# Unread matmuls placed ahead of six of TensorE's waits

## The chip, the cores and the metric

The kernel runs on one core of a Trainium2 chip (trn2). The metric is the device time of one execution in microseconds (us); lower is better. "PE" is TensorE's matmul queue, "PEld" its weight loads, DVE is VectorE, ACT is ScalarE, POOL is GpSimd and SPq the queue of transfers that SyncE issues.

## The reference, cut to what matters

The input is 16 batches of 512 tokens with 128 features. Three residual blocks follow each other; each starts with a layer norm.

- Block 1: linear attention with Chebyshev features. q, k, v = x W_in, clipped; polynomials of orders 1 to 5; running sums of T(k) v and of T(k) along the tokens; out = numerator / (denominator + 1e-7), times W_out.
- Block 2: a second layer norm, then ordinary causal softmax attention with 16 heads of 8 features, times Wp.
- Block 3: a gate picks 2 of 8 experts for each token; each expert is 128 to 512, exact gelu, 512 to 128; the two results are added with softmax weights.

```python
x = x + _L0_attn_ref(_layernorm(x), W_in, W_out)
x = x + _L0_ffn_ref(_layernorm(x), ...)      # softmax attention, then the experts
```

## The kernel before

All five engines run programs written out by hand, each a sequence of steps with waits on semaphores. An engine goes through its steps strictly in the written order.

**The pipeline over batches.** `pipelined(body)` runs `body` 21 times, t = -5 to 15. One pass works on up to six batches at once, each at another stage: `f` (block 1's norm and projections), `h` (its running sums and result), `g` (block 2's norm and projections), `m` (the row maxima of the scores), `b` (exp and the product with the values) and `t` (Wp, the gate, the dispatch to the experts). In the first five passes only some stages have a batch. This is the run-up: pass -5 has f only, pass -4 has h and f, pass -3 has g, h and f, pass -2 has m as well, and so on. Inside a pass TensorE's steps stand at 129 numbered places; `MAX_PE`, `SCORES_PE` and `VALUES_PE` list the places of the maxima, scores and value products.

**Steps of TensorE that matter here** (line numbers of the profile):

- `turn_h` (L1254, place 75): four transposes of the normed batch (L1243) into PSUM bank `front0`, behind a wait for the norm on DVE; then `project_k`, `project_q`, `project_v` (L1264, places 79 to 81): three f32 products of 128 x 512.
- `head_sums` (L1281, places 4 and 6, matmuls L1289): per-head sums of the k polynomials, then of the q polynomials. Both wait for POOL's even orders (`t24`, L1125 and L1126) and DVE's odd ones.
- `denominators` (L1293, place 51, matmuls L1297): eight matmul instructions of 16 columns; it waits for the fourth running sum on DVE. `turn_rden` (L1303), `spread_rden` (L1313) and `output1` (L1324) follow from it.
- `turn_ln`, `project_q2`, `project_k2`, `project_v2` (places 58 to 70, L1338 to L1346): block 2's projections.
- `maximum` (L1349, matmuls L1360 and the mask L1362): 44 steps for a batch (`NMAX` = 44), n = 0 to 43. Step 0 and step 22 (`NMAX // 2`) wait for a transfer that fills a half of the operand `stack`; the others wait until DVE has reduced the tile two steps back (L580). With `MAX_PE`, step 9 stands at place 39 and step 22 at place 83, two places behind `project_v`.
- `turn_x2` (L1434, place 25) and `gate` (place 31, L1441), then `ranks` (place 52, L1448 to L1452).
- After the 21 passes: a wait for the experts' plan and split weights, then `turn_in(0)` (four transposes L1243 of the first gathered block into `scores0`) and 39 expert blocks (`hidden` L1547, `output` L1559).

**Steps of DVE that matter here.** DVE's list `MAX_DVE` puts the reductions of steps 21, 22 and 23 one behind the other (slots 45 to 47); then come `third_order` (L513) and `fifth_order` (L517) of k, `max_rest` (L585), `ratio` (L561), and the other reductions. DVE too goes strictly in order.

The PSUM bank `scores1` (`ringE[1]`) is used by the scores and, later, by the experts' transposes.

Of the kernel before, what the change touches and what calls it, by code (L numbers as in the profile page):

```python
# [28 lines left out]
B, T = 16, 512  # L29
# [82 lines left out]
def block_kernel(nc, x, consts, cols, row_biases, w_in, w_out, wq, wk, wv, wp, gate_w, ew1, ew2, eb2, out):  # L112
    with ExitStack() as ctx:
        place = {}

        def sb(name, shape, dt=F32):
            tensor = ctx.enter_context(nc.sbuf_tensor(name, shape, dt))
            width = int(np.prod(shape[1:])) * (2 if dt == BF16 else 4)
            place[name] = nc.sbuf_base - -(-width // 32) * 32
            return tensor  # L120
# [22 lines left out]
        identb = sb("identb", [P, P], BF16)  # L143
        triu = sb("triu", [P, P], BF16)
        onesb = sb("onesb", [P, P], BF16)
        maskA = sb("maskA", [P, 4 * P], BF16)
# [111 lines left out]
        X, Y, Z, V = (ctx.enter_context(nc.psum_tensor(n, [P, T], F32)) for n in ("front0", "front1", "back0", "back1"))  # L258
        ringE = [ctx.enter_context(nc.psum_tensor(f"scores{i}", [P, T], F32)) for i in range(2)]
# [25 lines left out]
        NMAX = len(MAXIMA)  # L285
# [952 lines left out]
        def _(pe):  # L1238
            k = nc.tensor

            def turn(src, dst, done):
                for t in range(QT):
                    last = k.transpose(dst[:, t * P:(t + 1) * P], src(t), ident)  # L1243
                last.then_inc(done, 1)
# [6 lines left out]
            pe.wait_ge(W.const_ready, 4)  # L1251


            def turn_h(f, h, g):  # L1254
                pe.wait_ge(norm["a"]["out"], f * QT + QT)
                if g is not None:
                    pe.wait_ge(W.v_ev, g + 1)
                elif h is not None:
                    pe.wait_ge(W.rdT_ev, h + 1)
                turn(lambda t: hn[:, t, :], X, W.tr0)  # L1260
# [19 lines left out]

            def head_sums(f, z, dst, t24, t35, done, dst_read, upto):  # L1281

                if upto:
                    pe.wait_ge(dst_read, upto)
                pe.wait_ge(t24, f * 2 + 2)
                pe.wait_ge(t35, f * 2 + 2)
                for p in range(ORDERS):
                    j, var = (p, 0) if p < 4 else (0, 1)
                    last = k.matmul(dst[32 * j:32 * j + 32, :], cst[:, C_SUM + 32 * var:C_SUM + 32 * var + 32], z[p],  # L1289
                                    start=(p < 4), stop=(p > 0), skip_group_check=True)  # L1290
                last.then_inc(done, 1)

            def denominators(f):  # L1293
                pe.wait_ge(W.d_prod, f + 1)
                pe.wait_ge(W.kv_sum, f * ORDERS + 4)
                for t in range(QT):
                    last = k.matmul(X[:, t * H:(t + 1) * H], ksum[:, t * P:(t + 1) * P], cst[:, C_WS:C_WS + H],  # L1297
                                    start=True, stop=True)
                last.then_inc(W.den_mm, 1)
# [49 lines left out]
            def maximum(m, n, p):  # L1349

                head, heads, t = MAXIMA[n]
                if n in (0, NMAX // 2):
                    pe.wait_ge(stack_in[n // (NMAX // 2)], m * 32 + 32)
                if n == HALF_AT + 1:
                    pe.wait_ge(n2_ready[0], m + 1)
                elif n >= 2:
                    pe.wait_ge(W.smax_red, m * NMAX + n - (n != HALF_AT))
                for j in range(heads):
                    h, at = head + j, j * (t + 1) * P
                    k.matmul(ring(n)[:, at:at + (t + 1) * P], qst[p][0:MROW, h, t * P:(t + 1) * P],  # L1360
                             kst[p][0:MROW, h, 0:(t + 1) * P], start=(j == 0), stop=True, skip_group_check=True)
                k.matmul(ring(n)[:, 0:heads * (t + 1) * P].rearrange("p (h n) -> p h n", h=heads)[:, :, t * P:(t + 1) * P],  # L1362
                         identb[:, :], maskA[:, 0:heads * P].rearrange("p (h n) -> p h n", h=heads),
                         start=False, stop=True, skip_group_check=True).then_inc(W.smax_mm, 1)
# [67 lines left out]
                last.then_inc(W.o2_mm, 1)  # L1432

            def turn_x2(b):  # L1434
                pe.wait_ge(norm["b"]["out"], b * QT + QT)
                turn(lambda t: rows[:, 0, t, 0:D], Z, W.tr3)

# [25 lines left out]
            def body(t, b, m, g, h, f, p):  # L1463
# [3 lines left out]
                for n in range(SLOTS):  # L1467
                    at = lambda place, stage: n == place and stage is not None
                    if m is not None and n in MAX_PE:
                        maximum(m, MAX_PE.index(n), 1 - p)  # L1470
# [6 lines left out]
                    if at(4, h):  # L1477
                        head_sums(h, kx, X, W.k_t24, W.k_t35, W.ks_mm, W.x1_ready, h)
                    if at(6, h):
                        head_sums(h, qx, Y, W.q_t24, W.q_t35, W.qs_mm, *((W.x2_ready, t + 1) if t is not None else (W.outT_ready, h)))  # L1480
                    if at(25, t):
                        turn_x2(t)
                    if at(31, t):
                        gate(t)
                    if at(51, h):
                        denominators(h)
# [16 lines left out]
                    if at(75, f):  # L1503
                        turn_h(f, h, g)
# [21 lines left out]
            pipelined(body)  # L1526


            pe.wait_ge(W.plan_ready, 1)
            pe.wait_ge(W.wl_ready, 2 * E)  # L1530

# [76 lines left out]
```

## Time and profile before

| | |
|---|---|
| median of 3 runs | 1512.45 us (1511.88 to 1514.55) |
| the profiled execution | 1512.91 us |
| its span, first to last instruction | 1510.7 us |
| PE busy | 1260.2 us, 83% |
| DVE busy | 1167.6 us, 77% |
| ACT busy | 918.9 us, 61% |
| POOL busy | 854.2 us, 57% |
| chain that ended last | PE 61%, DVE 18%, issue 7%, ACT 6%, DMA 4%, POOL 3% |
| mean granted TensorE clock | 0.917 of full speed |

The chain is followed back from the last instruction, at each step to what released it; an engine's share of it is time that sets the end. The granted clock is 1.00 at 2.4 GHz and 0.50 at 1.2 GHz. A row of a timeline gives start, duration, engine, line, instruction, output and inputs, how many were merged, and in brackets the idle time of the engine before it with what ended it.

### The profile page before, as it was taken

What the parts mean: (1) busy time and instruction counts of PE and PEld (TensorE: products, weight loads), DVE (VectorE), ACT (ScalarE), POOL (GpSimd) and SP (SyncE); (2) the same over time, 40 slices, a digit from 0 to 9 for tenths busy, and PEclk for the clock granted to TensorE, in tenths of its full rate; (3) what the DMA queues carried; (4) which work ended last, traced back from release to release, by engine and by line L of the source; (5) the groups of instructions that cost most, each with busy time, mean ns of one, the idle gap of its engine ahead of it and who ended that gap; (6) DMA issues with size and microseconds to landing.
All of it is one profiled execution on the core that took longest, in us unless ns stands there. A gap on an engine that the chain in (4) does not pass through costs nothing.

```text
span 1510.7 us, 27693 instructions
## 1 busy us (share of the span) xinstructions
PE 1260.2 (83%) x8757; PEld 722.4 (48%) x8819; DVE 1167.6 (77%) x2654; ACT 918.9 (61%) x1794; POOL 854.2 (57%) x1077
## 2 busy tenths in 40 slices
PE   2545898999989999998999999989888199999970
PEld 0222354544545454454544545444445178888850
DVE  4548789888998988889898898875551578888864
ACT  1131376666767667675666766666545289999950
POOL 5567445766676666656766666552032326666660
PEclk9666799999999999999999999999999589999995
DMA  3012321404223141321403214043143022222238
GB/s 97 0 49 36 85 64 23 103 20 107 65 51 86 30 112 50 67 79 37 110 21 92 75 34 100 16 100 86 30 135 134 30 76 77 86 86 81 81 134 333
DMA packets 79345, 116.23 MB, mean 77 GB/s; under 512 B 15396, under 2 KB 61496, under 8 KB 74976
## 3 DMA queue, kind: packets, MB, share of 16 engines
q1 hardware_dynamic: 65888, 92.41, 23.4%
q0 software_dynamic: 9088, 17.33, 3.4%
q10 hardware_dynamic: 4224, 4.72, 1.0%
q8 instruction: 71, 1.16, 0.3%
q14 instruction: 74, 0.61, 0.1%
HBM read 58.29 MB, written 57.43 MB: 77 GB/s over the span
## 4 chain that ended last, share of the span: by engine, by line
PE 61%; DVE 18%; issue 7%; ACT 6%; DMA 4%; POOL 3%; SPq 1%; POOLq 0%; DVEq 0%; another core or an unknown queue 0%; ACTq 0%
DVE nm L580 9%; PE scores L1386 8%; PE front L1547 7%; PE back L1406 7%; PE back L1559 7%; PE maxima L1360 7%; PE front L1289 3%; PE front L1264 3%; ACT pr L963 3%; PE scores L1389 2%; PE back L1243 2%; PE maxima L1362 2%; DMA stack<-pairs 2%; DVE front L531 1%; PE front L1338 1%
## 5 line engine op out<-in xcount | busy, mean ns | idle before, releaser
L580 DVE TENSOR_REDUCE nm<-maxima 128x1 f32<-128x384 f32 (+3 forms) x704 | 427.7, 634 | 94.1 <-PE maxima L1362 67.3
L963 ACT ACTIVATE pr<-scores 128x384 f32<-128x384 f32 (+1 forms) x768 | 378.5, 524 | 186.4 <-PE scores L1389 172.3
L1360 PE MATMUL maxima<-stack 96*128 96x128 bf16 (+3 forms) x1024 | 258.2, 311 | 43.1 <-DVE nm L580 33.2
L1386 PE MATMUL scores<-stack 98*128 98x512 bf16 (+3 forms) x1024 | 260.7, 310 | 33.7 <-ACT pr L963 27.8
L1386 PEld LDWEIGHTS scores<-stack 98*128 98x128 bf16 x1024 | 91.7, 101 | 205.6 <-ACT pr L963 134.1
L1389 PE MATMUL scores<-maskB,identb 128*128 128x128 bf16 (+1 forms) x768 | 186.4, 243 | 0.0
L1406 PE MATMUL back<-pr,vaug 128*9 128x512 f32 (+3 forms) x2048 | 183.2, 454 | 0.0
L1164 POOL DMA_INDIRECT xg<-rows,sloti x128 | 129.9, 1014 | 88.4 <-DVE sloti L653 47.0
L1134 POOL TENSOR_TENSOR kv<-F,kv 128x512 f32<-128x512 f32 x80 | 112.5, 1418 | 116.2 <-DVE kv L534 116.2
L1360 PEld LDWEIGHTS maxima<-stack 96*128 96x128 bf16 x1024 | 85.8, 99 | 169.1 <-DVE nm L580 113.4
L1232 POOL DMA_INDIRECT pairs<-xs x104 | 111.0, 1067 | 78.8 <-DVE xs L814 52.0
L1362 PE MATMUL maxima<-maskA,identb 128*128 128x128 bf16 (+1 forms) x642 | 152.4, 237 | 0.0
L1547 PE MATMUL front<-h_first,w_now 128*128 128x512 f32 x312 | 126.3, 406 | 2.4 <-DVE h_second L794 2.4
L1099 ACT ACTIVATE xs<-front,b1p 128x512 f32<-128x512 f32 x156 | 107.4, 689 | 19.8 <-PE front L1547 16.7
L1125 POOL TENSOR_SCALAR F<-F 128x512 f32<-128x512 f32 x32 | 52.6, 1645 | 113.9 <-DVE F L513 113.9
L1559 PE MATMUL back<-hid_first,w_now 128*128 128x512 f32 x312 | 96.2, 390 | 0.0
L534 DVE TENSOR_TENSOR_SCAN kv<-one,front 128x512 f32<-128x512 f32 x80 | 95.2, 1206 | 0.1
L1145 POOL TENSOR_TENSOR kv<-kv 128x512 f32<-128x512 f32 x64 | 80.3, 1265 | 3.8 <-POOL kv L1145 0.4
L807 DVE TENSOR_TENSOR hid_second<-xs,hid_first 128x512 fp32r<-128x512 f32 x99 | 67.9, 686 | 15.6 <-ACT hid_first L1080 14.7
L1389 PEld LDWEIGHTS scores<-maskB,identb 128*128 128x128 bf16 x768 | 76.4, 99 | 6.9
L1080 ACT ACTIVATE hid_first<-xs 128x512 fp32r<-128x512 f32 x117 | 74.1, 633 | 3.7
L1362 PEld LDWEIGHTS maxima<-maskA,identb 128*128 128x128 bf16 x704 | 70.5, 100 | 8.7 <-issue 4.6
(223 smaller groups left out, 2491.7 us busy)
## 6 DMA issues: line engine op xcount, KB each, us to landing
stack<-spread SPq DMA_DIRECT2D x64, 384.0 KB, 6.4
spread<-qs SPq DMA_DIRECT2D x96, 128.0 KB
spread<-ks SPq DMA_DIRECT2D x96, 128.0 KB
xs<-xg SPq DMA_DIRECT2D x39, 272.0 KB, 2.9
stack<-pairs SPq DMA_DIRECT2D x8, 1024.0 KB, 16.6
xg<-xs SPq DMA_DIRECT2D x17, 272.0 KB
xs<-in_x SPq DMA_DIRECT2D x16, 256.0 KB, 5.8
acc<-xs SPq DMA_DIRECT2D x16, 256.0 KB, 2.3
```

What stands on the lines that cost most here:

```text
L580: v.tensor_reduce(nm[:, h:h + heads, t], ring(n)[:, 0:heads * (t + 1) * P].rearrange("p (h n) -> p h n", h=heads), AX.X, ALU.max, negate=T ...
L963: a.activation(pr[:, n % PR, 0:width], ringE[n % 2][:, 0:width], ACT.Exp).then_inc(W.exp_ready, 1)
L1134: g_.tensor_tensor(kv[:, p, :], qx[p], kv[:, p, :], ALU.mult).then_inc(W.qk_prod, 1)
L1164: g_.indirect_dma_start(xg[:, :], bass.IndirectOffsetOnAxis(sloti[:, i, q:q + 1], 0), rows[:, i, q, :], None).then_inc(W.dispatched, 16)
L1232: g_.indirect_dma_start(pairs[:, :], bass.IndirectOffsetOnAxis(xt[i % XT][:, at:at + 1].bitcast(U32), 0), yo[i % 3][:, q * D:(q + 1) * D], ...
L1360: k.matmul(ring(n)[:, at:at + (t + 1) * P], qst[p][0:MROW, h, t * P:(t + 1) * P], kst[p][0:MROW, h, 0:(t + 1) * P], start=(j == 0), stop=T ...
L1362: k.matmul(ring(n)[:, 0:heads * (t + 1) * P].rearrange("p (h n) -> p h n", h=heads)[:, :, t * P:(t + 1) * P], identb[:, :], maskA[:, 0:hea ...
L1386: k.matmul(dst[:, at:at + T - t * P], kst[p][0:MROW + 2, h, t * P:(t + 1) * P], qst[p][0:MROW + 2, h, t * P:T], start=(t == tiles[0]), sto ...
L1389: k.matmul(dst[:, 0:2 * P * many].rearrange("p (i n) -> p i n", i=many)[:, :, 0:P], identb[:, :], maskB[:, 0:many * P].rearrange("p (i n) ...
L1406: last = k.matmul(V[32 * i:32 * i + DH + 1, t * P:T], vaug[:, b % VR, t, 4 * (s_ // 3) + i, :], pr[:, (4 * s_ + i) % PR, at:at + T - t * P ...
L1547: last = k.matmul((X, Y)[n % 2][:, :], w_now[:, i % 2, wi, c * P:(c + 1) * P], h2p[hi][:, i % 2, :], start=(j == 0), stop=(j == len(TERMS3 ...
L1559: last = k.matmul((Z, V)[i % 2][:, :], w_now[:, i % 2, 2 + wi, c * P:(c + 1) * P], (hidh, hidl)[hi][i % 2 * HC + c], start=(c == 0 and j = ...
```

## The change

A helper `fill_in(many)` issues that many matmuls with no wait and no semaphore. Each multiplies `identb` (128x128 bf16) with `maskA` (128x512 bf16) into the bank `scores1`; nobody reads the results. It is called in six places of TensorE's program, each time ahead of the step's own waits:

- 12 in `turn_h` of batch 0,
- 20 ahead of the k sums of batch 0,
- 36 and 56 ahead of `denominators` of batches 0 and 1,
- 30 ahead of step 22 of `maximum` of batch 0,
- 24 in `turn_x2` of the last batch,
- 60 between the passes and the experts.

That is 238 matmuls in all. Nothing is removed and no other engine's program changes.

```diff
+            def fill_in(many):
+
+                for _ in range(many):
+                    k.matmul(ringE[1][:, :], identb[:, :], maskA[:, :], start=True, stop=True, skip_group_check=True)
+
             def turn_h(f, h, g):
+                if f == 0:
+                    fill_in(12)
                 pe.wait_ge(norm["a"]["out"], f * QT + QT)
...
             def head_sums(f, z, dst, t24, t35, done, dst_read, upto):
 
+                if f == 0 and dst is X:
+                    fill_in(20)
...
             def denominators(f):
+                if f < 2:
+                    fill_in(36 if f == 0 else 56)
                 pe.wait_ge(W.d_prod, f + 1)
...
             def maximum(m, n, p):
 
                 head, heads, t = MAXIMA[n]
+                if m == 0 and n == NMAX // 2:
+                    fill_in(30)
                 if n in (0, NMAX // 2):
                     pe.wait_ge(stack_in[n // (NMAX // 2)], m * 32 + 32)
...
             def turn_x2(b):
+                if b == B - 1:
+                    fill_in(24)
                 pe.wait_ge(norm["b"]["out"], b * QT + QT)
...
             pipelined(body)
 
+            fill_in(60)
             pe.wait_ge(W.plan_ready, 1)
```

## Rows read from the trace of the kernel before

**Rows 1.** Page, 40 slices of 37.8 us: PE busy and granted clock in tenths.

```profile
PE   2545898999989999998999999989888199999970
...
PEclk9666799999999999999999999999999589999995
```

**Rows 2.** Windows of 4 us in the run-up (DMA share, GB/s last).

```profile
42.00:46.00 4.00, 1.68 (x7) 0.26 (x2) 2.94 (x5) 0.00 (x0) 1.05 (x5) 0.97 0.00 0
46.00:50.00 4.00, 0.00 (x0) 0.00 (x0) 4.00 (x4) 0.00 (x0) 2.87 (x2) 0.89 0.01 2
...
82.00:86.00 4.00, 0.00 (x0) 0.00 (x0) 3.31 (x4) 0.83 (x3) 3.12 (x8) 0.65 0.00 0
...
122.00:126.00 4.00, 4.00 (x19) 0.78 (x14) 2.07 (x6) 0.69 (x2) 2.69 (x10) 0.73 0.02 2
...
130.00:134.00 4.00, 0.00 (x0) 0.00 (x0) 4.00 (x4) 1.10 (x3) 3.27 (x6) 0.63 0.00 0
```

**Rows 3.** Timeline of PE in the run-up: start us, us, instruction, idle before it.

```profile
22.82 1.09 PE L1243 MATMUL front<-cst,hn 128*128 128x128 f32 x4 [5.88 <-DVE hn L460]
25.95 5.49 PE L1264 MATMUL front<-hT,w_in_sb 128*128 128x512 f32 x6 [2.05 <-ACT hT L854]
37.91 5.76 PE L1289 MATMUL front<-F,cst 128*32 128x512 f32 x20 [6.47 <-POOL F L1126]
55.04 1.86 PE L1297 MATMUL front<-cst,ksum 128*128 128x16 f32 x8 [11.36 <-DVE kv L534]
...
60.52 5.49 PE L1264 MATMUL front<-hT,w_in_sb 128*128 128x512 f32 x6 [0.69 <-ACT hT L854]
...
94.98 1.86 PE L1297 MATMUL front<-cst,ksum 128*128 128x16 f32 x8 [16.38 <-DVE kv L534]
...
105.17 0.63 PE L1243 MATMUL front<-cst,hn 128*128 128x128 f32 x4 [1.00 <-ACT vaug L921]
...
139.90 0.61 PE L1360 MATMUL maxima<-stack 96*128 96x512 bf16 x1 [10.02 <-DVE nm L580]
...
153.56 2.94 PE L1264 MATMUL front<-hT,w_in_sb 128*128 128x512 f32 x6 [0.41 <-ACT hT L854]
```

**Rows 4.** Timeline of all engines, POOL's last even order of q.

```profile
39.29 1.48 POOL L1126 TENSOR_SCALAR F<-F 128x512 f32<-128x512 f32 x1
```

**Rows 5.** Timeline of PE in a later pass.

```profile
655.20 1.01 PE L1297 MATMUL front<-cst,ksum 128*128 128x16 f32 x8
```

**Rows 6.** The chain between 44 and 125 us, shares by line.

```profile
by line: issue 11.8%; DMA stack<-spread 9.0%; PE front L1264 6.8%; DVE hn L460 6.0%; PE front L1289 5.1%; DVE front L531 4.8%; PE front L1297 4.6%; DVE kv L534 3.2%; PE front L1243 2.7%; SPq L356 2.7%; POOL lnvm L420 2.6%; PE front L1324 2.
```

**Rows 7.** Timeline around maximum's step 22, PE and weight loads.

```profile
156.33 0.38 PE L1360 MATMUL maxima<-stack 96*128 96x512 bf16 x1
156.33 0.10 PEld L1362 LDWEIGHTS maxima<-maskA,identb 128*128 128x128 bf16 x1 [0.33 <-issue]
...
156.55 0.22 PE L1362 MATMUL maxima<-maskA,identb 128*128 128x128 bf16 x1
...
156.61 0.39 PE L1360 MATMUL maxima<-stack 96*128 96x128 bf16 x4
```

**Rows 8.** Timeline of DVE, the reductions of steps 22 and 23.

```profile
157.41 1.38 DVE L580 TENSOR_REDUCE nm<-maxima 128x4 f32<-128x512 f32 x2
```

**Rows 9.** Timeline of all engines at the last batch's gate.

```profile
1183.98 1.12 PE L1243 MATMUL back<-cst,rows 128*128 128x128 f32 x4 [9.54 <-ACT rows L454]
...
1184.96 0.61 ACT L984 ACTIVATE rows<-rows 128x512 f32<-128x512 f32 x1
...
1187.56 0.68 DVE L665 TENSOR_TENSOR w_second<-stack,w_first 128x512 fp32r<-128x512 f32 x1
1188.21 0.19 DVE L612 TENSOR_TENSOR lg<-back,row 128x32 f32<-128x32 f32 x1
```

**Rows 10.** Timeline, the experts' first transposes.

```profile
1208.99 1.09 PE L1243 MATMUL scores<-cst,xs 128*128 128x128 f32 x4 [17.54 <-DMA xs<-xg]
```

**Rows 11.** Window over the first eight microseconds of the experts.

```profile
1209.00:1217.00 8.00, 6.51 (x20) 4.82 (x20) 2.94 (x7) 3.88 (x7) 0.00 (x0) 0.53 0.78 233
```

## The prediction

> **What bounds the kernel.** I read the page's slices first, to see where PE waits and at which clock. From the sixth slice (189 us) on PE is busy eight or nine tenths at a clock of nine. The thin parts are the first four slices, with 2 to 5 tenths and clock digits of mostly 6, and the slice from 1171 us, with 1 tenth at a clock of 5; the fifth slice is busy, at a clock of 7 [rows 1]. The windows and the timeline then say how long each gap is, what stands behind it, and at which clock that work ran [rows 2, 3]. Last I read the chain that ended last, because only PE time that lies on it can shorten the kernel. PE has a large share of it, but in the run-up DVE's sums, POOL and transfers stand on it as well [rows 6].
>
> The rows hold each kind of work at both clock levels. Three projections take 5.49 us at 25.95 and 60.52 and 2.94 us at 153.56; four transposes 1.09 and 0.63 us [rows 3]; the denominators 1.86 us [rows 3] and 1.01 us in a later pass [rows 5]. So a slow clock costs 2.55, 0.46 and 0.85 us. That is what the fillers could win back.
>
> **When the clock moves, by rows.** The sums at 37.91 began at 1.2 GHz. The window from 42 us has a mean of 0.97, so the rise fell at about 42.2, 4.3 us after the work began. Falls: PE stopped at 43.67 (55.04 less its idle 11.36) and the 0.89 of the window from 46 us puts the fall at 49.1, 5.4 us later. It stopped at 78.60, and 0.65 puts the fall at 83.2, 4.6 us later. It stopped at 129.88, and 0.63 puts the fall at 131.0, only 1.2 us later, after a mixed stretch [rows 2, 3]. A filler train is thus worth something if it ends less than 1.2 us ahead of the real work, and perhaps nothing if it ends 5 us ahead.
>
> The Trainium skill (TensorE: Matmul & The Clock Gate, "What's actually happening") says the slow clock is the default, that activity releases it, and that where in a program this happens differs between runs. It adds that the ramp costs under 1% of a typical kernel's span. An estimate from that page is then under 15.1 us for all of it. The falls above agree that the moment varies.
>
> **What one filler costs.** The nearest row is a 512-column matmul of `maximum` at full clock: the matmul behind it starts 0.22 us later (156.33 to 156.55), and that one's weight load runs beside it [rows 7]. So a filler costs 0.22 us at full clock, and twice that, 0.43, at half. From below nothing supports less. From above, if the weight load did not hide, 0.10 us is added [rows 7].
>
> **Part by part.** Each train against its gap:
>
> - 12 ahead of the first transposes. PE is free from 16.94 [rows 3]; its last wait there ends some tenths later. At half clock 12 fillers take 5.2 us, with a rise after some 4.3 us a little less. They end near 22.0 and the transposes come at 22.82. No delay. The transposes run fast: 0.46 us won. Between them and the projections PE is idle for 2.05 us again [rows 3], so the clock may fall once more. If it holds, the projections win 2.55 us, if it falls, nothing or a quicker second rise. I take 1.2, about the middle.
> - 20 ahead of the k sums. The gap is 6.47 us [rows 3]. The clock is up, or comes up early in the train after 5.5 us of projections, so 4.4 to 6.1 us are used. No delay. The k and q sums take 5.76 us over both clocks. At full clock the k sums are done early, and the q sums wait for POOL, whose last q step ends at 40.77 [rows 4]. With the 1.88 us that ten of these instructions take at full clock (the 78.60 above is 76.72 and 1.88) they end at 42.65 instead of 43.67. Won: 1.0.
> - 36 and 56 ahead of the denominators. At full clock they take 7.9 and 12.3 us of gaps of 11.36 and 16.38 us [rows 3]. No delay, even if the first ten run slow (2.1 us more). They end 3.5 and 4.1 us ahead of the work, inside the 1.2 to 5.4 us in which a fall came. The denominators win 0.85 each if the clock holds. The projections behind the first come at 60.52, later still. I take 0.6 for the two and all behind them. The lower bound is nothing. The upper bound: PE's lines L1264, L1289, L1297 and L1243 hold 6.8, 5.1, 4.6 and 2.7% of the chain from 44 to 125 us [rows 6], 15.5 us of 81. At full clock all the way they would take about half, 7.8 us less.
> - 30 ahead of step 22. This is the part that costs. Step 22 is not behind an idle gap. It started at 156.61, right behind step 21's mask of 156.55, with no idle time [rows 7]. Its transfer had long landed: the DMA share is 0.02 from 122 us [rows 2]. The 10.02 us gap of this pass ends at 139.90 [rows 3], ahead of step 9, and gets no filler. So the 30 stand in PE's busy stretch: 30 x 0.22 = 6.6 us. Step 22's matmuls ended at 157.00 (156.61 and 0.39), and DVE took the tile at 157.41 [rows 8]. With 6.6 us more it takes it at 163.6, 6.2 us late; I take 6.0. Behind it on DVE wait the odd orders of k, the maxima's rest, the ratio of block 1 and every later reduction; behind the fillers on PE wait `turn_maxima`, `spread_rden` and `output1`. Both engines stop, and there is no third engine that sets the end here. What can come back is a clock that stays up longer: slice five shows 7 tenths [rows 1], but behind the train the same thin mix runs that let it fall before. The bounds are 4.0 (some of the slow stretch won back) and 8.1 (a clock at half for the first ten fillers).
> - 24 ahead of the last gate's transposes. The gap is 9.54 us; the train takes 5.3 at full and about 7.4 with a slow start. No delay. The transposes end at 1185.10 instead of perhaps 1184.6, but ScalarE is busy with the rows' copy until 1185.57 (1184.96 and 0.61), and DVE with a weight split until 1188.24 (1187.56 and 0.68) ahead of the gate's first step [rows 9]. Faster PE work here is covered by both. Worth nothing, costs nothing.
> - 60 ahead of the experts. The gap is 17.54 us, ended by the gathered block [rows 10]. With ten slow the train takes 15.3 us and ends at about 1206.8, 2.2 ahead of the transposes at 1208.99, where 0.46 us is to be won. In the eight microseconds from 1209 the mean clock is 0.53 and PE is busy for 6.51 us [rows 11]; were all of it at full speed, up to 3.1 us would go. Another idle step separates transposes and first products, so I take 0.5.
>
> Sum against the profiled execution: 1512.91 + 6.0 - (0.46 + 1.2 + 1.0 + 0.6) - 0.5 = 1515.15; I say 1515.0. The profiled execution is 0.46 us above the median of the runs.
>
> **The rivals.**
>
> - *The clock stays up from train to train* (ends on the other side). For it: a fall came 5.4 us after a stop [rows 2, 3], longer than any rest that the trains leave. Against it: the fall after 1.2 us. All of it held: 0.46 + 2.55 + 1.0 + 7.8 in the run-up and 3.1 at the experts, 14.9 in all, gives 1512.91 + 6.0 - 14.9 = 1504.0; half of what is open gives about 1508. It decides the sign from 6.0 us won on, and shows as faster from 9.0. Chance 0.15.
> - *The 30 cost less than their time*, because the clock stays up behind them and PE, which waits in turns with DVE, catches up by 2 us or more; with a little more held elsewhere: 1509.5 to 1513. Chance 0.18.
> - *The 30 or the weight loads cost more.* If the clock is low when the 30 begin, 8.1 instead of 6.0: 1517.1. If each filler also pays its weight load, it costs 0.32: the 30 take 9.6, 3.0 more, and the 56 take 17.9, over their gap by 1.5: 1512.91 + 9.0 + 1.5 - 3.3 - 0.5 = 1519.6. Against it: the overlap in [rows 7]. The Trainium skill (same page, Part 3, "What overlaps and what doesn't") says that a weight load overlaps running matmuls only where the row group differs, which would make each filler pay it. The trace disagrees, since here both use all rows or nearly so. Chance of the two together 0.17.
> - *The fillers do nothing*: every train but the 30 ends too early and the clock falls each time. 1512.91 + 6.0 less only the 0.46 and 1.0 that stand right behind trains: 1517.5. It is counted in my own case's upper end.
>
> **How the numbers follow.** My own case, 1513 to 1517.5, has 0.50. A measurement of this kernel tells about 0.2%, 3.0 us, from no change: faster is below 1509.4, slower above 1515.5. My own case lies with 0.30 under that upper bound and 0.20 above it; the cheaper 30 is nearly all within; the dearer case is above it; the held clock gives 0.13 faster. Together: faster 0.14, the same 0.49, slower 0.37. The range reaches from 1508.0 (half the held clock) to 1518.5 and leaves out about one in ten on each side at most.
>
> **What the next profile would show.** Right: 238 more PE matmuls on one line; before step 22 of `maximum` a train of 6.6 us and a DVE idle time of about 6 us ended by PE at L580, followed by work shifted as a whole; the q sums end about 42.7 less what was won before; the fourth DVE sum still ends the wait of both denominators; the gate's first DVE step still starts right behind a weight split. Wrong: projections of 2.9 us at both early places, denominators of 1.0 us in passes -4 and -3, first expert products 0.23 us apart from the start; or a train of 0.3 us a filler; or step 22's train in front of an idle DVE that had other work to do.

## The result: slower by 0.46%

The changed kernel takes 1519.0 us in the median of 13 runs (1513.05 to 1522.82), the kernel before in the same comparison 1511.88 us (13 runs, 1508.94 to 1521.99). The ratio is 1.0046, 95% interval 1.0034 to 1.0059, so 7.0 us slower (5.1 to 8.9). I forecast 1515.0 and a range up to 1518.5: the sign of my own case was right, the size was not, and the time lies just outside the range.

The profiled execution after took 1522.45 us (span 1520.2), among the longest of its runs. The page's slices, PE and clock, answer to [rows 1]:

```profile
PE   4776899999999899999999999989898889999970
...
PEclk9776799999999999999999999999988799999995
```

PE is busier in the first four slices and around 1190 us. The clock digits there rise by none, one or two.

The timeline of PE in the run-up of the changed kernel, the lines that answer to [rows 3]:

```profile
17.37 5.14 PE L1257 MATMUL scores<-maskA,identb 128*128 128x512 bf16 x12 [0.39 <-DVE row L491]
22.77 0.66 PE L1243 MATMUL front<-cst,hn 128*128 128x128 f32 x4 [0.26 <-DVE hn L460]
25.48 4.54 PE L1271 MATMUL front<-hT,w_in_sb 128*128 128x512 f32 x6 [2.05 <-ACT hT L854]
29.86 4.48 PE L1257 MATMUL scores<-maskA,identb 128*128 128x512 bf16 x20
36.62 1.90 PE L1298 MATMUL front<-F,cst 128*32 128x512 f32 x10 [2.28 <-POOL F L1126]
39.53 1.90 PE L1298 MATMUL front<-F,cst 128*32 128x512 f32 x10 [1.00 <-POOL F L1126]
41.36 7.94 PE L1257 MATMUL scores<-maskA,identb 128*128 128x512 bf16 x36
52.80 1.73 PE L1308 MATMUL front<-cst,ksum 128*128 128x16 f32 x8 [3.49 <-DVE kv L534]
...
58.15 5.33 PE L1271 MATMUL front<-hT,w_in_sb 128*128 128x512 f32 x6 [0.69 <-ACT hT L854]
...
76.01 12.26 PE L1257 MATMUL scores<-maskA,identb 128*128 128x512 bf16 x56
92.47 1.86 PE L1308 MATMUL front<-cst,ksum 128*128 128x16 f32 x8 [4.20 <-DVE kv L534]
```

L1257 is the train. All of these end inside their gaps: the bracket of the line behind each is the idle time that is left. The first projections take 4.54 instead of 5.49 us, the q sums end at 41.43 instead of 43.67. But the trains of 36 and 56 end 3.5 and 4.2 us ahead of the denominators, and these take 1.73 and 1.86 us, hardly less than the 1.86 of before; the second projections take 5.33 instead of 5.49. Those 92 fillers bought next to nothing.

The same timeline at step 22, answering to [rows 7]:

```profile
153.35 0.38 PE L1373 MATMUL maxima<-stack 96*128 96x512 bf16 x1
153.57 0.22 PE L1375 MATMUL maxima<-maskA,identb 128*128 128x128 bf16 x1
153.63 6.64 PE L1257 MATMUL scores<-maskA,identb 128*128 128x512 bf16 x30
160.10 0.39 PE L1373 MATMUL maxima<-stack 96*128 96x128 bf16 x4
```

And DVE there, answering to [rows 8]; the bracket is its idle time:

```profile
153.83 0.69 DVE L580 TENSOR_REDUCE nm<-maxima 128x1 f32<-128x512 f32 x1 [0.18 <-PE maxima L1375]
160.75 1.29 DVE L580 TENSOR_REDUCE nm<-maxima 128x4 f32<-128x512 f32 x2 [6.22 <-PE maxima L1375]
```

PE goes from step 21 straight into the train; DVE sits idle for 6.22 us for step 22. The chain that ended last runs through the train itself (start, us, what):

```profile
153.52 0.22 PE maxima L1373
153.74 0.06 PE maxima L1375
153.79 6.47 PE scores L1257 x30
160.27 0.23 PE maxima L1373 x4
...
160.75 1.29 DVE nm L580 x2
```

The last gate and the experts' first transposes, answering to [rows 9] and [rows 10]:

```profile
1193.99 0.66 PE L1243 MATMUL back<-cst,rows 128*128 128x128 f32 x4 [1.16 <-ACT rows L454]
...
1194.98 0.61 ACT L984 ACTIVATE rows<-rows 128x512 f32<-128x512 f32 x1
...
1197.57 0.69 DVE L665 TENSOR_TENSOR w_second<-stack,w_first 128x512 fp32r<-128x512 f32 x1
1198.17 0.18 DVE L612 TENSOR_TENSOR lg<-back,row 128x32 f32<-128x32 f32 x1
...
1219.08 0.63 PE L1243 MATMUL scores<-cst,xs 128*128 128x128 f32 x4 [2.05 <-DMA xs<-xg]
```

The gate's transposes take 0.66 instead of 1.12 us and nobody gains: ScalarE's copy still ends behind them (1195.59 against 1194.65), and the gate's first DVE step still starts right behind the weight split.

### The profile page after: what moved, and what is told of

The parts are those of the page before. It is cut to its first block, busy times and chain, and to the rows that moved or that the text cites. A ratio compares the mean times of both kernels' runs of the same rounds, so it can differ in the third digit from the quotient of the medians.

```text
span 1520.2 us, 28231 instructions
## 1 busy us (share of the span) xinstructions
PE 1327.2 (87%) x9057; PEld 748.7 (49%) x9057; DVE 1165.8 (77%) x2654; ACT 919.3 (60%) x1794; POOL 852.3 (56%) x1077
## 4 chain that ended last, share of the span: by engine, by line
PE 62%; DVE 16%; issue 6%; ACT 6%; DMA 4%; POOL 4%; SPq 1%; POOLq 0%; DVEq 0%; ACTq 0%
PE scores L1399 8%; PE back L1419 8%; DVE nm L580 7%; PE front L1563 7%; PE back L1575 7%; PE maxima L1373 7%; ACT pr L963 3%; PE front L1271 3%; PE front L1298 3%; PE scores L1402 3%; PE maxima L1375 2%; PE back L1243 2%; DMA stack<-pairs 2%; DVE hn L460 1%; DVE front L531 1%
## 5 line engine op out<-in xcount | busy, mean ns | idle before, releaser
L1375 PE MATMUL maxima<-maskA,identb 128*128 128x128 bf16 (+2 forms) x704 | 177.2, 252 | 0.0
```

## The experiments

The theories before the first one. A: the train of 30 costs the time that it holds PE's queue, the others win a little, and effects add. B: the 30 also slow the later passes. C: other trains cost something. The later expectations name their own theories. Each kernel was compared with the kernel before on its own chip, whose median is given; the six chips had medians from 1512 to 1560 us, so ratios are compared, not times.

**Only the 30.** The calls of 12, 20, 36/56, 24 and 60 are taken out.

```diff
-                if f == 0:
-                    fill_in(12)
...
-                if f == 0 and dst is X:
-                    fill_in(20)
...
-                if f < 2:
-                    fill_in(36 if f == 0 else 56)
...
                 if m == 0 and n == NMAX // 2:
                     fill_in(30)
...
-                if b == B - 1:
-                    fill_in(24)
...
-            fill_in(60)
```

> Only the train of 30 ahead of step 22 is kept; the other five call sites are gone. Theory A (the train costs its own time on the PE and DVE path, everything else in the result is the luck of the clock in the steady passes): about 6 us over the kernel before, near 1518; DVE's first denominators (L556) of passes -4 to -2 at the same time as before, the fourth one 6 us later, and that difference stays within 1.5 us until the end. Theory B (the train, or the shift that it brings, also makes the later passes slower): 8 us or more over before, with the lag growing from pass to pass. Theory C (the train costs little and the other trains cost the rest): under 4 us.

Measured: 1.0045 (1.0030 to 1.0059), before 1550.01 us. That is nearly all of the loss by one call. The lag was read from DVE's reciprocals of the denominators (L556), one in each pass; step 22 lies between the third and the fourth. From the third to the fourth this kernel took 66.79 us, the one with the two last trains alone, on the same chip, 60.54. Against that kernel it was 2.2 us late at the third, 8.5 at the fourth, 10.6 at the fifth and 7.0 at the sixteenth. Theory B's lag that grows from pass to pass is not there, though theory A's 1.5 us of play was too narrow.

**All but the 30.**

```diff
-                if m == 0 and n == NMAX // 2:
-                    fill_in(30)
```

> All of the change but the 30 ahead of step 22. Theory A: about 3.5 us faster than before (3.0 in the run-up, some tenths at the experts), near 1508.4. Theory B puts the trouble on the 30 alone: the same 3.5 us. Theory C (trains elsewhere cost something later, for example a clock that falls more often in the steady passes): no faster than before.

Measured: 0.9989 (0.9977 to 1.0000). As one number it is 1.7 us, half of the 3.5 expected, and its interval reaches no gain at all.

**Only the four early trains** (12, 20, 36, 56).

> Only the trains of 12, 20, 36 and 56. Theory A: 3.0 us faster than before, all of it gained ahead of 145 us (L556 2.4, 2.5 and 3.0 us early) and then carried unchanged to the end. Theory C: the lead is lost again in the steady passes.

Measured: 0.9999 (0.9987 to 1.0011). Expected 0.998: a miss. In its profile and in that of the next kernel the passes keep the same distance, some 2.0 us, from the third reciprocal (141.00 and 143.04) on to 1163 us, so no lead is lost in the later passes there. But that execution was the fastest of its 12 (1545.37 us, median 1549.18), and the median shows no gain.

**Only the two last trains** (24 and 60).

> Only the trains of 24 (last gate) and 60 (ahead of the experts). Theory A: 0.5 us faster at most, not to be told from before; the gate's first DVE step still starts right behind a weight split, the experts' first transposes take 0.63 instead of 1.09 us. Theory C: up to 2 us slower, if PE's reads slow the engines that make the plan.

Measured: 0.9993 (0.9982 to 1.0005). No cost, and no gain that can be told from none.

**The change again, beside its parts**, unaltered, on another chip.

> The change itself, unaltered, beside its parts on one chip. Only the 30 gave a ratio of 1.0045, all but the 30 gave 0.9989: if parts add, the whole is 1.0034, near 5.2 us. Theory A (parts add; the rest of the 7.1 us first measured is scatter): 1.003 to 1.004. Theory B (the whole is dearer than its parts, through the clock of the later passes): 1.005 or more.

Measured: 1.0046 (1.0027 to 1.0065), before 1512.01 us. The first result stands. As one number it lies between the two theories, 1.003 to 1.004 and 1.005 or more, and its interval holds both.

**The 30 moved to step 9**, which stands behind the 10 us gap; the other trains stay.

```diff
-                if m == 0 and n == NMAX // 2:
+                if m == 0 and n == 9:
                     fill_in(30)
```

> The change with the 30 moved from step 22 to step 9 of maximum, the one that stands behind the 10 us gap; the other trains stay. 30 fillers take 6.6 us of that gap. Theory A (place decides, not number): no cost left, 1 to 2 us faster than before like the kernel without the 30, a little more if the clock is still up at step 9. If fillers cost time anywhere, through memory or the clock: still 4 us or more slower than before.

Measured: 1.0001 (0.9981 to 1.0020). The same number of fillers, 13 steps earlier, and the loss is gone. The gain that theory A expected on top does not show. PE's timeline has the train inside its gap, with 3.40 us of it left:

```profile
127.36 6.64 PE L1257 MATMUL scores<-maskA,identb 128*128 128x512 bf16 x29
137.40 0.39 PE L1373 MATMUL maxima<-stack 96*128 96x512 bf16 x1 [3.40 <-DVE nm L580]
```

The place decides.

**60 and 15 instead of 30 at step 22**, no other train.

```diff
-                    fill_in(30)
+                    fill_in(60)
```

> Only a train of 60 ahead of step 22, twice the length, no other train. Theory A (each filler costs its own 0.22 us there, less 0.4 of slack once): 6.5 us more than with 30, 12.8 to 13.4 us over before. A cost that is mostly a fixed loss by a later clock: 8 to 10 us.

> Only a train of 15 ahead of step 22. Theory A: 15 x 0.22 less 0.4 of slack, 2.9 us over before. If a fixed loss comes with the shift itself (later passes lose 1 to 4 us by the clock whatever the length): 4 to 6 us.

Measured: 1.0108 (1.0080 to 1.0136) with 60 and 1.0026 (1.0006 to 1.0045) with 15, that is 16.3 (12.1 to 20.6) and 3.9 (0.9 to 6.8) us. PE's train of the 60 in the profile (two records of it are missing):

```profile
154.78 12.90 PE L1257 MATMUL scores<-maskA,identb 128*128 128x512 bf16 x58
```

The loss grows with the train's length; a loss that is mostly fixed is out. The direct loss is read best from DVE's reciprocals. From the third to the fourth the profiles of all kernels show (us):

```
no train at step 22   60.54 to 61.92 (eleven kernels, mean 60.86)
15 fillers            63.38
30 fillers            66.68, 66.79, 66.62, 66.68, 67.59, 67.74
60 fillers            73.37
26 thin matmuls       69.37
```

Over the mean of 60.86 that is 2.5, 6.2 (mean of six), 12.5 and 8.5 us; compared chip by chip the 30 cost 6.2 us on the one where they took 67.59 and 67.74 (61.06 and 61.92 without), and 6.0 on the others. I had forecast 6.0 for the 30. By time the 60 lost 16.3 us, 3.8 more than those 12.5; its interval reaches down to 12.1.

**A train of the same length that streams hardly any columns**: 26 f32 matmuls of one column.

```diff
-                    fill_in(30)
+                    for _ in range(26):
+                        k.matmul(ringE[1][:, 0:1], ident, col[:, V_B2:V_B2 + 1], start=True, stop=True)
```

> No fillers; ahead of step 22 stand 26 f32 matmuls of one column each, whose time is weight loads. The nearest rows of such instructions took 0.13 us at full and 0.17 to 0.23 us at half clock, two instructions a matmul, so the train takes 6.5 to 8.6 us at about the length of the 30, but hardly streams any columns. Theory A (the loss is the time that PE's queue is held, nothing else): 6 to 8 us over before, as with the 30. A theory in which dense fillers themselves do the harm (memory, power, clock afterwards) expects much less, one in which they help expects 1 to 2 us more than with the 30.

Measured: 1.0080 (1.0054 to 1.0106), 12.4 us (8.4 to 16.5) on a chip with 1557.86, more than the 6 to 8 us of theory A. PE's timeline and two windows of 4 us (the clock is the third number from the end):

```profile
155.22 6.59 PE L1359 MATMUL scores<-col,cst 128*128 128x1 f32 x52
```

```profile
156.00:160.00 4.00, 4.00 (x38) 4.00 (x38) 0.11 (x1) 1.53 (x3) 0.00 (x0) 1.00 0.70 159
160.00:164.00 4.00, 3.54 (x20) 2.75 (x20) 1.27 (x3) 0.03 (x1) 0.00 (x0) 0.53 0.99 152
164.00:168.00 4.00, 3.64 (x16) 2.58 (x17) 3.29 (x7) 0.93 (x3) 3.18 (x2) 0.50 0.81 122
```

The same windows of the kernel with only the 30:

```profile
156.00:160.00 4.00, 4.00 (x20) 1.81 (x19) 1.12 (x2) 2.75 (x6) 0.00 (x0) 1.00 0.54 162
160.00:164.00 4.00, 3.85 (x23) 1.79 (x20) 0.44 (x1) 0.00 (x0) 0.00 (x0) 1.00 1.11 178
164.00:168.00 4.00, 2.69 (x19) 1.83 (x20) 3.98 (x9) 0.53 (x2) 2.39 (x2) 1.00 1.02 145
```

PE is busy in both, but the clock falls while the thin train still runs and is at half behind it; behind the dense one it is full until 168. The other profiles agree: with the 30 the clock fell between 167.5 and 171.9 us in six kernels, with no train at step 22 between 157.0 and 163.1 in nine of eleven, with the thin train at 160.3. So the dense fillers do keep the clock up for what follows them, worth 8.5 - 6.2 = 2.3 us here, by one profile of the thin train; they pay for it with 6.5. Of the 12.4 us, 3.9 don't stand in that profile between the third and the fourth reciprocal and stay unexplained.

**Longer trains that reach the work behind them**, none at step 22 or at the last gate.

```diff
-                    fill_in(36 if f == 0 else 56)
+                    fill_in(50 if f == 0 else 72)
...
+                if m == 0 and n == 9:
+                    fill_in(44)
...
-            fill_in(60)
+            fill_in(70)
```

> Longer trains that reach nearly to the work behind them, and none at step 22 nor at the last gate: 12, 20, 50 and 72 ahead of the two denominators, 44 at step 9 behind the 10 us gap, 70 ahead of the experts. At 0.22 us they take 11.0 of 11.4, 15.8 of 16.4, 9.7 of 10.0 and at most 17.2 of 17.5 us. If the clock then stays up, the denominators take 1.01 instead of 1.86 us, and the projections behind them 2.9 instead of 5.5: 4 to 8 us faster than before. If the clock falls all the same in the thin work behind each train: 1 to 3 us faster. If a train overruns its gap: 1 to 2 us slower than that.

Measured: 0.9998 (0.9979 to 1.0017), against the 4 to 8 us faster of the first case. Yet its profile shows what was hoped for:

```profile
41.43 10.74 PE L1257 MATMUL scores<-maskA,identb 128*128 128x512 bf16 x49 [0.16 <-issue]
52.65 1.04 PE L1308 MATMUL front<-cst,ksum 128*128 128x16 f32 x8 [0.48 <-DVE kv L534]
...
57.24 4.29 PE L1271 MATMUL front<-hT,w_in_sb 128*128 128x512 f32 x6 [0.69 <-ACT hT L854]
...
121.30 11.35 PE L1257 MATMUL scores<-maskA,identb 128*128 128x512 bf16 x43
```

The denominators take 1.04 us, and the third reciprocal comes at 137.84, against a mean of 144.1 in eight kernels without early trains. That is a lead of 6 us in this execution, and none in the median of the runs. This execution was the fastest of its 12 (1551.84 us, median 1556.74). The last line shows one thing that can go wrong: at step 9 the 44 took 11.35 us, more than the 10 us gap, since the clock was at 0.50 from 122 to 124 us. DVE then sat idle for 1.15 us until PE had done step 9.

**No 30, and only the 30, once more**, on that same chip.

> The change without the 30, unaltered, on another chip. Its denominators of pass -2 came 2.4 us earlier than those of kernels without early trains (means of five profiles each). Theory A (what is won there arrives at the end): 0.9980 to 0.9985. A theory in which it is lost again in later passes: 1.000.

> Only the 30, unaltered, beside the kernel without it. The profiles show 6.1 us lost up to the next pass. Theory A (that is all): 1.0040. A theory of a further loss in the later passes: 1.0050 or more, and low-clock stretches in each pass that the kernel without the 30 does not have.

Measured: 0.9978 (0.9957 to 0.9998) and 1.0040 (1.0020 to 1.0061). Both agree with theory A; the second interval holds the other theory's 1.0050 as well.

**Four more, on what stayed open.** One train of 44 at step 9 alone; only the two denominators' trains at 50 and 72; the change without 24 and 60; the long version with the 30 put back at step 22.

> One train alone, 44 at step 9 of maximum, 9.7 us in a gap of 10.0, so that nothing behind it starts later. In the profile of the long version the denominators behind it took 1.04 instead of 1.86 us. Theory D (the time of trains shows up one for one in the whole): 1 us faster to no change. Theory E (a train early in the program makes the later passes lose 2 to 4 us by whatever way): 1.001 to 1.003.

> Only the trains ahead of the two denominators, at 50 and 72. By the rows of the long version they win the denominators (0.8 us each), the transposes and part of the projections behind them: 4 us ahead of before at 145 us. Theory D: 0.997 to 0.998. Theory E: the lead is in the trace at 145 us and the whole is at 1.000.

> The change without its two last trains (24 and 60). They ended 1.2 and 2.1 us ahead of the work and won 0.3 us by the rows. Theory D: as the parts say, 6.1 less 2.4, 1.0025. If the two last trains are what makes the whole dearer than its parts: also 1.0025, but then the change beside it at 1.0046. Theory E: 1.004 to 1.005.

> The long version (12, 20, 50, 72, 44 at step 9, 70) with the 30 ahead of step 22 put back. The long version gave 0.9998. If the 30 cost the same 6.1 us on top of any other trains: 1.0038. If trains add to each other's cost: 1.005 or more.

Measured, before 1513.64 us: 1.0022 (1.0012 to 1.0032), 0.9997 (0.9974 to 1.0020), 1.0037 (1.0024 to 1.0049) and 1.0029 (1.0014 to 1.0044).

- The train of 44 alone costs 3.3 us (1.8 to 4.8), against theory D's forecast of none; theory E's range holds it.
- The two denominators' trains at 50 and 72 win nothing in the median. This is what theory E said, though the interval reaches theory D's 0.998 too. The profile, near its median (1515.26 us, median 1513.93), has the third reciprocal at 139.17, 6.4 us ahead of the kernel before (145.53), and the sixteenth at 976.85, against 976.80. Of the lead 1.4 us were lost up to the fourth reciprocal and 5.0 behind it.
- Without the 24 and 60 the ratio is 1.0037, between theory D's 1.0025 and theory E's 1.004, and the interval holds both. Together with 0.9993 for these two alone, nothing says that they make the change dear.
- The 30 cost 1.0029 against 0.9998 on the long base, some 4.7 us (1 to 8): no sign that they cost more there.

**The last two:** 30 at step 9 alone, and no call at all.

> One train alone, 30 at step 9, at most 8.7 us even with ten slow ones, in a gap of 10 us: it can't hold up step 9. Theory F (what e13 lost is its own train of 44, which fits its gap only at full clock: 9.7 us of 10.0 in two profiles, 11.35 in a third): no loss here, 0.999 to 1.001. Theory E (any train early on makes later passes lose): 1.0015 to 1.003.

> No train at all: the helper is defined and never called, so the instructions are those of the kernel before. Whatever this differs from before is what the comparison itself adds. Theory E and F: 1.000 within 0.001. If it comes out at 1.001 to 1.002, the excess of 1 to 3 us seen over the traces' own differences is no property of the trains.

Measured: 0.9997 (0.9980 to 1.0014) and 0.9995 (0.9972 to 1.0017), before 1560.33 us. The comparison shows no offset of its own, though its interval reaches 1.0017, and a train that has room in its gap costs nothing that shows. That leaves the overrun as the likely cause for the 44: it fits only at full clock. This is argued, not shown: in the profile of that kernel the train took 9.66 us and fitted, and that execution was the fastest of its runs.

## Why the prediction was wrong in size

**What held.** The place of the 30 (in PE's busy stretch, the 10 us gap being that of step 9), the price of a filler (6.47 us for 30, 0.22 each), its hidden weight load, the idle DVE (6.22 us), and the sum for it: 6.0 forecast, 6.2 in the mean of six profiles, and by time 1.0045 and 1.0040, weighted by their intervals 1.0043, or 6.5 us (4.7 to 8.4). With a weight load of 0.10 us ahead of each it would have been 9.6 us. The Trainium skill (TensorE: Matmul & The Clock Gate, "What overlaps and what doesn't") says that a load overlaps running matmuls only where the row group differs; the 6.47 us contradict that sentence here, since both operands use all rows. No cost for 24 and 60 shows, and nothing was won at the gate, as forecast. At the experts 0.3 us were won of the 0.5 forecast: from the last gate's slots (L651) to the first expert products 19.20 instead of 19.52 us; in the eight profiles with a train there it is 19.03 to 19.47, in the twelve without 19.43 to 19.63.

**What failed** is the other term of the sum, "(0.46 + 1.2 + 1.0 + 0.6)" and 0.5, 3.8 us to be won: it was sized at more than twice what came. By time the change without the 30 wins 0.9989, 0.9978 and, with 30 at step 9, 1.0001; weighted 0.9989, so 1.6 us (0.3 to 3.0). The kernel with the four early trains alone, 0.9999, is not in that mean; with it, it would be 1.1 us. Two things were wrong in the term. I measured the run-up against one profiled execution, and it was the latest of its kind there: its third reciprocal came at 145.53, those of eight kernels without early trains between 143.04 and 145.53, mean 144.1. Six kernels with the change's four early trains had it between 140.70 and 143.63, mean 142.1. So the mean lead was 2.0 us, not the 3.3 forecast. And the 0.6 for the denominators' trains was not there: they end 3.5 and 4.2 us too early. At the first reciprocal the mean lead of the same kernels was already 2.1 us (54.3 against 56.5): of the 2.7 us forecast for the trains of 12 and 20 most came, and nothing was added behind.

**The rest.** I forecast 6.0 - 3.8 = 2.2 us and 7.0 were measured. Of the missing 4.8 us, 2.2 are the won term and 0.5 the 30. The remaining 2.1 are open: 6.5 - 1.6 = 4.9 us is what the parts give, 5.6 us is what the change without its last two trains measured, and 7.0 us, twice, is what the whole measured. The parts' sum is uncertain by 2.2 us and the whole by some 1.5, so they don't contradict each other. No run shows a loss by the two last trains, by an early train with room in its gap, or an offset of the comparison, but the intervals leave room for up to 0.8, 2.2 and 2.7 us of them. The profiles show where an execution can lose such an amount. The first one of the changed kernel ended 9.5 us behind that of the kernel before, and 5.4 of them arose between the sixteenth reciprocal and the last gate's slots (220.68 against 215.25 us), long behind the trains of the run-up; the one of the repeat took 214.87 us there and ended 4.5 us behind, which is the parts' sum.

Also open is why the long version, 6 us ahead in its profile, is no faster in the median. The kernel with only 50 and 72 shows one way: its lead was gone by the sixteenth reciprocal, and from the fourth to the sixteenth its clock was low in 14 separate places, against 10 in the kernel before. Whether a lead brings such falls or they came by chance, one execution of each doesn't show.

**The range.** It ended at 1518.5 because I let the case of a dearer train stand for everything above my own. It lacked the plain error of the won term (from 3.8 down to nothing, which alone reaches 1518.9) on top of that. The measured 1519.0 lies among the times of that dearer case, but its mechanism wasn't there: the clock was at full and the loads were hidden, the 30 took 6.47 us. That case was also priced too low, since at 0.32 us a filler the 60 would have taken 19.2 us, 1.7 over their gap. And "half of what is open" doesn't give 1508: half of the way from 1515.15 to 1504.0 is 1509.6. Neither slip decided anything.

## What to carry to other kernels

A filler on an engine that works in order is free only if the engine is idle at that very place of its program, and long enough for the train at either clock; that the overrun at half clock is what the train of 44 paid for is likely, not shown. Look up the step behind the gap by its idle row and count the steps; here the gap belonged to step 9 and the train stood at step 22. And size what a clock trick may win against several executions, not the profiled one: the clock rises and falls at other moments in each.

## What the runs showed of the hardware that I had not expected

**The clock falls a different number of times in each execution.** Between the fourth and the sixteenth reciprocal, where all kernels run the same instructions, two windows (of the kernel with 44 at step 9 alone, and of that with 50 and 72 alone), on one chip:

```profile
205.00:972.00 767.00, 712.25 (x5578) 364.05 (x5624) 674.00 (x1603) 507.28 (x1068) 494.66 (x669) 0.98 0.28 66
```

```profile
201.00:977.00 776.00, 721.33 (x5583) 368.56 (x5629) 673.13 (x1605) 507.26 (x1068) 495.15 (x670) 0.97 0.27 65
```

The same stretch of work took 767.3 and 775.8 us; the clock was low in 8 and in 14 separate places. DVE, ACT and POOL were busy for the same time within 1 us, PE for 9 us more. That is 1.4 us a fall between these two. Over the ten profiles of the chips near 1512 us, with 7 to 14 low places and 767.3 to 775.9 us, it is 1.1 us a fall. The 8.5 us are more than all the run-up trains won. The runs without a profile show the same: in 29 executions of the kernel before on one chip the time went from 1505.40 us at a mean clock of 0.922 to 1523.43 at 0.909. That where the clock moves varies from run to run is also what the Trainium skill (same page, "What's actually happening") says.

**A higher mean clock is not less time.** The profiled execution of the changed kernel had a mean clock of 0.926 and took 1522.45 us, the kernel before 0.917 and 1512.91. That mean includes the time of the trains; what counts is the clock under the work that others wait for.

**The clock fell while PE was busy.** Under the thin train PE was busy for all of 158 to 162 us, and the granted clock was 1.00 in the first two of them and 0.57 in the last two. Under the dense trains of 30 at this place it stayed at full.

**Chips differ.** The kernel before took 1511.9, 1512.0 and 1513.6 us on three of them and 1550.0, 1557.9 and 1560.3 on the three others. Most of it lies late: two kernels with no train at step 22, that with only the two last trains on a slow chip and that with the 30 at step 9 on a quick one, were 0.3 us apart at the reciprocal of the third denominators (143.04 against 142.76) and 30 us apart at the last gate (its slots, L651, at 1220.06 against 1189.82). The cause was not looked for.
